# Attention scores and context as 32 by 32 products in runs, in place of block-diagonal 128 by 128 products between projections

## The chip, the core and the metric

The kernel runs on one core of one Trainium2 chip. The metric is the device time of one execution in microseconds; before the change it is 1934.57 (median of three runs, 1934.41 to 1936.26). A core has TensorE (matmuls, and weight loads that the trace keeps apart as PEld), VectorE (DVE), ScalarE (ACT), GpSimd (POOL) and SyncE (SP, which issues DMAs).

## The reference

One layer over 2048 tokens of width 1024, in float32. Attention is inside each token, between its 32 heads of 32 numbers; the feed-forward part has weights that are first rounded to a 16-level code per block of 64.

```
x = hidden                                   # (1, 2048, 1024)
n = layernorm(x)
q, k, v = ((n @ w.T + b).reshape(1, 2048, 32, 32) for w, b in ((wq, bq), (wk, bk), (wv, bv)))
scores  = einsum('bshd,bstd->bsht', q, k) / sqrt(32)
context = einsum('bsht,bstd->bshd', softmax(scores), v)
x = x + context.reshape(x.shape)
h = silu(n2 @ dq(w1).T) * (n2 @ dq(w2).T)    # n2 = layernorm(x), dq: NF4 quantize and dequantize, 2752 rows
x = x + h @ dq(w3).T
```

So each token has two products of 32 by 32 matrices: the scores (32 heads by 32 heads) and the context.

## The kernel before, in words

The 2048 tokens are 16 tiles of 128 (T = 16). After a stage that turns the attention weights (to 65 us), a step per tile runs the attention stage (to about 550 us), and the feed-forward stage follows to the end. Of a step n, TensorE first projects tile n on Q, K and V (`project_one`, m = 0, 1, 2). Each projection is two halves of 512 columns, and each half is 16 float16 matmuls of 128x512 (L1104: 8 parts of the width, times the high and the low part of the normalized x). Between Q and K it turns the next tile's x (`turn`, eight float32 transposes, L281). The same step does the attention of tile n - 1: `score_part` (L1144) and `mix_part` (L1156).

VectorE's 32-by-32 transposes lay a tile out so that each quadrant of 32 partitions holds one token's 32 by 32 matrix, 4 tokens at a time, 32 times (QUAD = 32 slots t, in two halves of 16, HALF). Before the change, ScalarE copies the 4 matrices of a slot from qT, or from the flipped exponentials, to the diagonal blocks of a zeroed 128 by 128 matrix `diag[:, t]` (`place`, L1000, called by `place_q` and `place_probs`: 4 copies per half, one per quadrant). One float32 matmul with that matrix as weights and the slot's kT (or vT) as 32 moving columns then does 4 tokens. GpSimd clears diag once.

The order on each engine is written out by hand. TensorE's small products stand one by one behind the big matmuls: `between` in `project_one` spreads the 32 scores over Q's 32 matmuls, the first 16 mixes over K's second half, and the other 16 over V's first half. Counters (semaphores) carry the waits: q_placed and p_placed from ScalarE, k_ready and v_ready from VectorE, scores_done and context_done back. Scores and contexts use the same two banks of PSUM, so a half's scores also wait until the context before was read (ctx_read).

VectorE evacuates each projection half (L802), subtracts the maxima (L939, L941), flips the exponentials (L956), turns q, k and v (L868, L886, L928), weighs and flips the context (L916, L923), does both layer norms' statistics, and looks for maxima of the feed-forward weights. ScalarE also makes the exponentials (L1048), the high parts of x (L287, L1068) and the first levels of the feed-forward weights' code (L1041, L1043).

The steps are: two written out, a loop of six iterations with two steps each, two more written out (in which the feed-forward stage's first work is fed in, `feed` and `ahead`), and a tail. In the tail the last tile's attention stands among the first feed-forward matmuls (L1907): `attend_last(slot)` is called behind each of 96 of them, and puts the scores at slots 0 to 31 and the mixes at slots 40 to 71 (MIX_FROM = 40). C is 8.

Of the kernel before, what the change touches and what calls it, by code (L numbers as in the profile page):

```python
# [24 lines left out]
P = 128  # L25
QUAD = 32
# [149 lines left out]
def attention(nc, g):  # L176
# [13 lines left out]
    with ExitStack() as mine:  # L190
# [327 lines left out]
        diag = sb("diag", [P, QUAD, P])  # L518
# [7 lines left out]
        diag_zero = sem("diag_zero")  # L526
# [3 lines left out]
        q_placed = sem("q_placed")  # L530
# [6 lines left out]
        p_placed = sem("p_placed")  # L537
# [48 lines left out]
        MIX_FROM = 40  # L586
# [133 lines left out]
        def gpsimd(pool, feed):  # L720
# [69 lines left out]
            pool.memset(diag[:], 0.0).then_inc(diag_zero, 1)  # L790
            straight_steps(step, tail, feed)

        def vector(dve, feed):
# [25 lines left out]
            def step(n, u, it, project=True, normalize=True, attend=True, end=True, feed=None, ahead=None):  # L819
# [44 lines left out]
                if project:  # L864
                    dve.wait_ge(evacuated, 6 * n + 2)
                    if not (it is None and n == 0):
                        dve.wait_ge(q_placed, 2 * n)
                    nc.vector.transpose(qT[:].rearrange("p t h u -> p h t u"),  # L868
                                        qkv[:].rearrange("p (h d) -> p h d", d=HD)).then_inc(q_ready, 1)
# [125 lines left out]
        def scalar(act, feed):  # L995
            def place(half, compact, done):

                part = slice(half * HALF, (half + 1) * HALF)
                for rows in quadrants:
                    last = nc.scalar.activation(diag[rows, part, rows].rearrange("p (t u) h -> p t u h", u=2),  # L1000
                                                compact[rows, half * HALF // 2:(half + 1) * HALF // 2], ACT.Copy)
                last.then_inc(done, 1)

            def step(n, u, it, project=True, normalize=True, attend=True, end=True, feed=None, ahead=None):
                if attend:
                    make_level(n, 0)
                    exponential(n, 0)
                    place_probs(n, 0, end)
# [10 lines left out]
                if attend:  # L1019
                    place_probs(n, 1, end)  # L1020
# [4 lines left out]
                if project:  # L1025
                    place_q(n, 0, attend)
# [4 lines left out]
                if project:  # L1031
                    place_q(n, 1, attend)
# [17 lines left out]
            def place_probs(n, half, end):  # L1050
                act.wait_ge(p_ready, 2 * n + half - 1)
                act.wait_ge(scores_done, 2 * n + half - 1)
                place(half, flipped[:].rearrange("p (t u h) -> p t u h", u=2, h=HEADS), p_placed)

            def place_q(n, half, attend):
                if half == 0:
                    act.wait_ge(q_ready, n + 1)
                if attend:
                    act.wait_ge(context_done, 2 * n + half - 1)
                else:  # L1060
                    act.wait_ge(diag_zero, 1)
                place(half, qT[:].rearrange("p t h u -> p t u h"), q_placed)

# [6 lines left out]
            def tail(feed):  # L1070
                next(feed)
                exponential(T, 0)
                halve2(T - 2)
                place_probs(T, 0, True)
                next(feed)
                exponential(T, 1)
                next(feed)
                place_probs(T, 1, True)
                next(feed)
                halve2(T - 1)  # L1080
                next(feed)
# [3 lines left out]
        def tensor(pe, feed_program):  # L1085
            def project_one(n, u, it, m, with_lo, between=None, share=(0, 2), halfway=None):


                for h in range(2):
                    i = 2 * m + h  # L1090
                    if h == 1 and halfway:
                        next(halfway)
# [10 lines left out]
                    for j, (x, w) in enumerate(passes):  # L1103
# [3 lines left out]
                        slot, slots = h * len(passes) + j, 2 * len(passes)  # L1107
                        if between and share[0] * slots <= 2 * slot < share[1] * slots:
                            between((2 * slot - share[0] * slots) * HALF // slots, (2 * slot + 2 - share[0] * slots) * HALF // slots)

            def step(n, u, it, project=True, normalize=True, attend=True, end=True, feed=None, ahead=None,
                         with_lo=False):
                def score(first, last):
                    score_part(n, end, first, last)

                def mix(first, last):
                    mix_part(n, first, last)

                def mix_second(first, last):
                    mix_part(n, HALF + first, HALF + last)  # L1120
# [13 lines left out]
            def score_part(n, end, first, last):  # L1134

                for t in range(first, last):
# [11 lines left out]
            def mix_part(n, first, last):  # L1148

                for t in range(first, last):  # L1150
# [834 lines left out]
```

## Time and profile before

| | |
|---|---|
| median of three runs | 1934.57 us |
| the profiled execution's own time | 1933.85 us |
| its span in the trace | 1932.1 us |
| TensorE matmuls / weight loads busy | 1883.0 / 1053.0 us |
| VectorE, ScalarE, GpSimd busy | 1730.8, 1542.4, 1256.0 us |
| mean granted TensorE clock | 0.992 |

Matmuls are pipelined: one is recorded from its start to a modelled end, so that neighbours overlap, and the time that one costs the engine is the distance between starts. A timeline row puts neighbouring instructions of one line together (x8) and gives the time from the first one's start to the last one's end. Start times are from the span's start. A loop's or a helper's instructions all have one line.

### The profile page before, as it was taken

What the parts mean: (1) busy time and instruction counts of PE and PEld (TensorE: products, weight loads), DVE (VectorE), ACT (ScalarE), POOL (GpSimd) and SP (SyncE); (2) the same over time, 40 slices, a digit from 0 to 9 for tenths busy, and PEclk for the clock granted to TensorE, in tenths of its full rate; (3) what the DMA queues carried; (4) which work ended last, traced back from release to release, by engine and by line L of the source; (5) the groups of instructions that cost most, each with busy time, mean ns of one, the idle gap of its engine ahead of it and who ended that gap; (6) DMA issues with size and microseconds to landing.
All of it is one profiled execution on the core that took longest, in us unless ns stands there. A gap on an engine that the chain in (4) does not pass through costs nothing.

```text
span 1932.1 us, 30875 instructions
## 1 busy us (share of the span) xinstructions
PE 1883.0 (97%) x10326; PEld 1053.0 (55%) x10326; DVE 1730.8 (90%) x1848; ACT 1542.4 (80%) x1779; POOL 1256.0 (65%) x707
## 2 busy tenths in 40 slices
PE   6899999999989999999999999999999999999998
PEld 5688888888764344444444444444444444444443
DVE  6789888888878999999999999999999999999995
ACT  7366757667568899898898998989989899898881
POOL 0134434343464797887877878778788797786971
PEclk9999999999989999999999999999999999999999
DMA  8435545455286422122122122122122122122114
GB/s 316 142 110 171 166 153 177 137 185 155 79 245 157 143 50 61 44 51 58 43 55 54 43 56 50 46 49 60 43 49 60 43 49 60 43 50 55 39 28 186
DMA packets 252861, 181.69 MB, mean 94 GB/s; under 512 B 177792, under 2 KB 220800, under 8 KB 252800
## 3 DMA queue, kind: packets, MB, share of 16 engines
q1 hardware_dynamic: 221600, 167.28, 30.9%
q10 hardware_dynamic: 31200, 13.64, 2.9%
q8 instruction: 33, 0.54, 0.1%
q14 instruction: 28, 0.23, 0.0%
HBM read 114.29 MB, written 24.12 MB: 72 GB/s over the span
## 4 chain that ended last, share of the span: by engine, by line
PE 64%; DVE 1%; issue 0%; DMA 0%; ACT 0%; SPq 0%; POOL 0%; DVEq 0%
PE bank L1907 42%; PE bank L1935 7%; PE bank L1936 7%; PE bank L1937 7%; PE bank L1933 0%; PE bank L1932 0%; DVE bank L1746 0%; DMA w3T_lo<-half 0%; DVE acc L1811 0%; DVE bank L1744 0%; SPq L1396 0%; DVE w_first L1746 0%; ACT half L1625 0%; ACT signs L1612 0%; DVE hidden L1754 0%
## 5 line engine op out<-in xcount | busy, mean ns | idle before, releaser
L1746 DVE SCALAR_TENSOR_TENSOR bank<-signs,bank 128x1024 f32<-128x1024 int8 (+2 forms) x756 | 920.3, 1217 | 54.6 <-ACT signs L1612 27.9
L1907 PE MATMUL bank<-x2T,w12T 128*128 128x512 f16 x4128 | 906.2, 380 | 11.9 <-DMA x2T<-x_lo_dram 9.0
L1907 PEld LDWEIGHTS bank<-x2T,w12T 128*128 128x128 f16 x4128 | 410.1, 99 | 493.3 <-DMA x2T<-x_lo_dram 9.2
L1612 ACT ACTIVATE signs<-w_first,compare_bias 128x1024 int8<-128x1024 f32 (+1 forms) x588 | 630.6, 1138 | 2.4 <-DVE bank L1746 1.9
L1612 ACT ACTIVATE signs<-w_last,compare_bias 128x1024 int8<-128x1024 f32 (+2 forms) x294 | 314.5, 1119 | 0.8 <-DVE w_first L1746 0.6
L1104 PE MATMUL bank<-wT,xT_hi 128*128 128x512 f16 x768 | 292.2, 381 | 2.4 <-PEq L321 2.4
L1104 PE MATMUL bank<-wT,xT_lo 128*128 128x512 f16 x768 | 292.0, 380 | 0.0
L1935 PE MATMUL bank<-w3T_hi,hT_hi 128*128 128x512 f16 x672 | 255.5, 380 | 7.3 <-DVE acc L1811 4.1
L1936 PE MATMUL bank<-w3T_lo,hT_hi 128*128 128x512 f16 x672 | 255.4, 380 | 0.0
L1937 PE MATMUL bank<-w3T_hi,hT_lo 128*128 128x512 f16 x672 | 255.3, 380 | 0.0
L1526 POOL TENSOR_TENSOR acc<-acc,hidden 128x512 f32<-128x512 f32 x160 | 200.8, 1271 | 28.0 <-ACT hidden L1653 27.2
L1144 PEld LDWEIGHTS bank<-kT,diag 128*128 128x128 f32 x1024 | 173.8, 194 | 15.7
L1653 ACT ACTIVATE hidden<-bank,un_scale 128x512 f32<-128x512 f32 x160 | 109.3, 683 | 87.9 <-PE bank L1937 66.1
L1156 PEld LDWEIGHTS bank<-vT,diag 128*128 128x128 f32 x1024 | 170.3, 190 | 15.0
L1811 DVE SCALAR_TENSOR_TENSOR acc<-bank,un_scale,acc 128x512 f32<-128x512 f32 x192 | 143.4, 747 | 22.6 <-PE bank L1933 11.5
L1520 POOL TENSOR_TENSOR hT_lo<-hidden,hT_hi 128x512 f16<-128x512 f32 (+1 forms) x88 | 101.7, 1157 | 87.7 <-ACT hT_hi L1642 85.1
L1144 PE MATMUL bank<-kT,diag 128*128 128x32 f32 x1024 | 157.8, 236 | 0.0
L1493 POOL TENSOR_SCALAR step_part<-w_first 128x1024 f32<-128x1024 f32 (+1 forms) x42 | 152.4, 3628 | 8.0 <-POOL w_last L1506 2.9
L1156 PE MATMUL bank<-vT,diag 128*128 128x32 f32 x1024 | 155.6, 233 | 0.0
L1502 POOL TENSOR_TENSOR w_first<-w_first,step_part 128x1024 f32<-128x1024 f32 (+1 forms) x42 | 99.0, 2358 | 77.2 <-DVE w_first L1746 77.1
L1104 PEld LDWEIGHTS bank<-wT,xT_hi 128*128 128x128 f16 x768 | 113.0, 147 | 36.2 <-issue 2.5
L1104 PEld LDWEIGHTS bank<-wT,xT_lo 128*128 128x128 f16 x768 | 114.4, 149 | 30.4
(143 smaller groups left out, 2352.2 us busy)
## 6 DMA issues: line engine op xcount, KB each, us to landing
ff_raw<-in_L_ffn_w SPq DMA_DIRECT2D x63, 512.0 KB, 4.5
w_first<-in_L_ffn_w SPq DMA_DIRECT2D x41, 512.0 KB, 3.9
w_last<-in_L_ffn_w SPq DMA_DIRECT2D x19, 512.0 KB, 3.9
x_nat<-in_L_attn_hidden_states SPq DMA_DIRECT2D x16, 512.0 KB, 5.4
x_res<-in_L_attn_hidden_states SPq DMA_DIRECT2D x16, 512.0 KB, 4.6
x<-x_res SPq DMA_DIRECT2D x16, 512.0 KB, 3.0
acc<-x SPq DMA_DIRECT2D x4, 2048.0 KB, 9.1
out<-acc SPq DMA_DIRECT2D x15, 512.0 KB, 2.6
```

The source lines that it names most:

```text
L1104: ins = nc.tensor.matmul(to, x, w, start=j == 0, stop=j == len(passes) - 1)
L1144: ins = nc.tensor.matmul(scores_of(n)[:, t], diag[:, t], kT[:, t // 2, :, t % 2], start=True, stop=True)
L1156: ins = nc.tensor.matmul(context_of(n)[:, t], diag[:, t], vT[:, t // 2, :, t % 2], start=True, stop=True)
L1493: nc.gpsimd.tensor_scalar(step_part[0:rows, 0:cols], w_nat(slot)[0:rows, 0:cols], float(BOUNDS[APART]), 2 * HALF_STEP[APART], ALU.is_gt, A ...
L1526: nc.gpsimd.tensor_tensor(acc[:, st, BANK:], acc[:, st, BANK:], hidden[:, st % 2], ALU.add).then_inc(summed, 1)
L1612: nc.scalar.activation(signs[0:rows, ring(v, k), 0:cols], w_nat(v % SLOTS)[0:rows, 0:cols], ACT.Sign, scale=COMPARE[SUMMED[k]][0], bias=co ...
L1746: V.scalar_tensor_tensor(to, part, HALF_STEP[SUMMED[k]], total, ALU.mult, ALU.add).then_inc(sign_used, 1)
L1811: V.scalar_tensor_tensor(acc[:, st, cols], down_bank(st, h), un_scale[:, 2:3], acc[:, st, cols], ALU.mult, ALU.add).then_inc(down_read[h], 1)
L1907: last = nc.tensor.matmul(dst, w, x[:, toks, c], start=c == 0 and i == 0, stop=c == C - 1 and i == 2)
L1935: nc.tensor.matmul(dst, hT_hi[k, p, toks], w3T_hi[k, p, cols], start=p == 0, stop=False)
L1936: nc.tensor.matmul(dst, hT_hi[k, p, toks], w3T_lo[k, p, cols], start=False, stop=False)
L1937: last = nc.tensor.matmul(dst, hT_lo[k, p, toks], w3T_hi[k, p, cols], start=False, stop=p == GROUP - 1)
```

## The change

Four things change.

1. A slot's product is 4 matmuls, one for each quadrant of 32 partitions, with the quadrant's 32 by 32 matrix of qT (or of the flipped exponentials) as weights, straight from where VectorE left it. `diag`, `place`, `place_q`, `place_probs`, the clearing of diag and the counters q_placed, p_placed and diag_zero go. TensorE waits for q_ready, p_ready and centered in their place.
2. The products are no longer spread between big matmuls. A half's 16 slots are one run of 64 matmuls: the first scores ahead of Q, the second in Q's middle, the first mixes in K's middle, the second behind K.
3. In the tail the scores' halves stand at slots 0 and 8, the mixes' at slots 40 and 56.
4. VectorE's transpose of q waits for no placing.

```diff
-            def place(half, compact, done):
-
-                part = slice(half * HALF, (half + 1) * HALF)
-                for rows in quadrants:
-                    last = nc.scalar.activation(diag[rows, part, rows].rearrange("p (t u) h -> p t u h", u=2),
-                                                compact[rows, half * HALF // 2:(half + 1) * HALF // 2], ACT.Copy)
-                last.then_inc(done, 1)
...
                 if project:
                     pe.wait_ge(x_lo_done, 2 * n + 2)
-                    project_one(n, u, it, 0, with_lo, score if attend else None, (0, 2))
+                    if attend:
+                        score_part(n, end, 0, HALF)
+                    project_one(n, u, it, 0, with_lo, score_second if attend else None)
                 if normalize:
                     pe.wait_ge(normed, n + 2)
                     turn(x_nat[:, 1 - u], x_turned)
                 if project:
-                    project_one(n, u, it, 1, with_lo, mix if attend else None, (1, 2))
-                    project_one(n, u, it, 2, with_lo, mix_second if attend else None, (0, 1), ahead)
+                    project_one(n, u, it, 1, with_lo, mix_first if attend else None)
+                    if attend:
+                        mix_part(n, HALF, QUAD)
+                    project_one(n, u, it, 2, with_lo, ahead_half if ahead else None)
...
-                    if t % HALF == 0:
-                        pe.wait_ge(q_placed, 2 * n + half - 1)
+                    if t == 0:
+                        pe.wait_ge(q_ready, n)
                     if t % HALF == 0 and end and scores_of(n) is scores:
                         pe.wait_ge(ctx_read, 2 * n + half - 3)
-                    ins = nc.tensor.matmul(scores_of(n)[:, t], diag[:, t], kT[:, t // 2, :, t % 2], start=True, stop=True)
+                    if t % HALF == 0:
+                        pe.sem_inc(held, 1)
+                    for rows in quadrants:
+                        ins = nc.tensor.matmul(scores_of(n)[rows, t], qT[rows, t // 2, :, t % 2], kT[rows, t // 2, :, t % 2], start=True, stop=True)
...
                     if t % HALF == 0:
-                        pe.wait_ge(p_placed, 2 * n + half - 1)
-                    ins = nc.tensor.matmul(context_of(n)[:, t], diag[:, t], vT[:, t // 2, :, t % 2], start=True, stop=True)
+                        pe.wait_ge(p_ready, 2 * n + half - 1)
+                        pe.wait_ge(centered, 2 * n + half - 1)
+                    if t % HALF == 0:
+                        pe.sem_inc(held, 1)
+                    for rows in quadrants:
+                        ins = nc.tensor.matmul(context_of(n)[rows, t], flipped[rows, t * HEADS:(t + 1) * HEADS], vT[rows, t // 2, :, t % 2],
+                                               start=True, stop=True)
...
-                    if slot < QUAD:
-                        score_part(T, True, slot, slot + 1)
-                    elif MIX_FROM <= slot < MIX_FROM + QUAD:
-                        mix_part(T, slot - MIX_FROM, slot - MIX_FROM + 1)
+                    if slot in LAST_SCORES:
+                        score_part(T, True, LAST_SCORES.index(slot) * HALF, (LAST_SCORES.index(slot) + 1) * HALF)
+                    elif slot in LAST_MIXES:
+                        mix_part(T, LAST_MIXES.index(slot) * HALF, (LAST_MIXES.index(slot) + 1) * HALF)
```

TensorE at the start of a step inside the loop, before: a weight load goes with each matmul and has no row of its own; L1104 is a projection, L1144 a score.

```order
L1104 MATMUL bank<-wT,xT_hi 128x512 [waits evacuated]
L1141 REGISTER_ALU [waits k_ready]
L1143 REGISTER_ALU [waits q_placed]
L1144 MATMUL bank<-kT,diag 128x32 [waits ctx_read]
L1104 MATMUL bank<-wT,xT_lo 128x512
```

The same place after the change (L1110 is a score, L1066 a projection):

```order
L1106 REGISTER_ALU [waits q_ready,k_ready,x_lo_done]
L1110 MATMUL bank<-kT,qT 32x32 [waits ctx_read]
L1110 MATMUL bank<-kT,qT 32x32 x63
L1058 ISA
L1066 MATMUL bank<-wT,xT_hi 128x512 [waits evacuated]
L1066 MATMUL bank<-wT,xT_lo 128x512
```

Sixteen products that stood between the first half's matmuls of Q are one block of 64 rows ahead of them all.

TensorE in K's middle and behind K, after the change (L1126 is a mix):

```order
L1121 REGISTER_ALU [waits v_ready]
L1126 MATMUL bank<-vT,flipped 32x32 [waits p_ready,centered]
L1126 MATMUL bank<-vT,flipped 32x32 x63
L1066 MATMUL bank<-wT,xT_hi 128x512 [waits evacuated]
...
L1066 MATMUL bank<-wT,xT_lo 128x512
L1126 MATMUL bank<-vT,flipped 32x32 [waits p_ready,centered]
L1126 MATMUL bank<-vT,flipped 32x32 x63
L1058 REGISTER_ALU
```

The second half's mixes stood in V's first half and are now ahead of V.

ScalarE in one step before, from the first exponential to the first level:

```order
L1048 ACTIVATE probs<-probs 128x512 [waits centered]
L1000 ACTIVATE diag<-flipped 32x16x32 [waits scores_done,p_ready]
L1000 ACTIVATE diag<-flipped 32x16x32 x3
L287 ACTIVATE xT_hi<-bank 128x512 [waits x_turned] x2
L1048 ACTIVATE probs<-probs 128x512 [waits centered]
L1068 ACTIVATE x_half<-x_res 128x1024 [waits normed2]
```

And after the change:

```order
L1026 ACTIVATE probs<-probs 128x512 [waits centered]
L287 ACTIVATE xT_hi<-bank 128x512 [waits x_turned] x2
L1026 ACTIVATE probs<-probs 128x512 [waits centered]
L1032 ACTIVATE x_half<-x_res 128x1024 [waits normed2]
```

The copies are gone, and all else keeps its order.

## Rows read from the trace of the kernel before

**Rows 1.** The page: busy us (share) and instructions, and the clock in 40 slices.
```profile
PE 1883.0 (97%) x10326; PEld 1053.0 (55%) x10326; DVE 1730.8 (90%) x1848; ACT 1542.4 (80%) x1779; POOL 1256.0 (65%) x707
...
PEclk9999999999989999999999999999999999999999
```
**Rows 2.** Sums over five steps of 30.67 us, one from 301.44: busy, and means.
```profile
sum 153.35, PE 153.35 PEld 126.19 DVE 135.49 ACT 101.58 POOL 63.83; mean PE 30.67 PEld 25.24 DVE 27.10 ACT 20.32 POOL 12.77
```
**Rows 3.** Groups by line and shape: busy us, mean ns, idle before.
```profile
L1144 PE MATMUL bank<-kT,diag 128*128 128x32 f32 x1024 | 157.8, 236 | 0.0
```
**Rows 4.** Timeline of TensorE inside Q of one step: start us, length us.
```profile
301.80 0.38 PE L1104 MATMUL bank<-wT,xT_lo 128*128 128x512 f16 x1
302.01 0.30 PE L1144 MATMUL bank<-kT,diag 128*128 128x32 f32 x2
302.15 0.38 PE L1104 MATMUL bank<-wT,xT_hi 128*128 128x512 f16 x1
...
302.51 0.38 PE L1104 MATMUL bank<-wT,xT_lo 128*128 128x512 f16 x1
```
**Rows 5.** Timeline of TensorE in streams of one shape.
```profile
72.27 1.04 PE L281 MATMUL bank<-ident,x_nat 128*128 128x128 f32 x8
73.15 0.38 PE L1104 MATMUL bank<-wT,xT_hi 128*128 128x512 f16 x1
60.05 1.06 PE L463 MATMUL bank<-wT 128*128 128x128 f16 x16
62.74 0.16 PE L506 MATMUL bank<-ones,lo_sum 128*1 128x1 f32 x1 [0.70 <-DVE lo_sum L428]
62.74 0.19 PE L506 MATMUL bank<-ones,lo_sum 128*1 128x1 f32 x2 [0.70 <-DVE lo_sum L428]
```
**Rows 6.** Timeline where weights of another height follow, and where not (28.33).
```profile
28.33 0.22 PE L463 MATMUL bank<-wT 128*128 128x128 f16 x1
28.33 0.08 PEld L469 LDWEIGHTS bank<-ident,qkv_top 128*1 128x1 f32 x1
29.76 0.22 PE L463 MATMUL bank<-wT 128*128 128x128 f16 x1
29.91 0.18 PEld L473 LDWEIGHTS bank<-scale_row,ones 1*128 1x128 f32 x1
12.32 0.25 PE L473 MATMUL bank<-scale_row,ones 1*128 1x2 f32 x1
12.49 0.14 PEld L486 LDWEIGHTS bank<-ident,w_raw 128*128 128x128 f32 x1
```
**Rows 7.** Groups by line and shape: ScalarE's copies into diag.
```profile
L1000 ACT ACTIVATE diag<-qT 32x512 f32<-32x512 f32 x128 | 86.1, 673 | 5.5 <-PE bank L1156 2.4 <-DVE qT L868 2.0
L1000 ACT ACTIVATE diag<-flipped 32x512 f32<-32x512 f32 x128 | 80.3, 628 | 56.7 <-DVE flipped L956 36.6 <-issue 18.9
```
**Rows 8.** Timeline of TensorE in the tail.
```profile
551.47 0.38 PE L1907 MATMUL bank<-x2T,w12T 128*128 128x512 f16 x1
569.24 0.61 PE L1907 MATMUL bank<-x2T,w12T 128*128 128x512 f16 x1 [9.04 <-DMA x2T<-x_lo_dram]
588.23 15.70 PE L1907 MATMUL bank<-x2T,w12T 128*128 128x512 f16 x72
```
**Rows 9.** Timeline of VectorE in the step from 301.44.
```profile
312.82 0.70 DVE L956 STREAM_TRANSPOSE flipped<-probs 128x512 f32<-128x512 f32 x1
317.96 0.70 DVE L956 STREAM_TRANSPOSE flipped<-probs 128x512 f32<-128x512 f32 x1
325.45 1.25 DVE L886 STREAM_TRANSPOSE kT<-qkv 128x1024 f32<-128x1024 f32 x1
```
**Rows 10.** Stretch of the lower clock: length, busy of PE, PEld, DVE, ACT, POOL, clock, DMA, GB/s.
```profile
561.80:575.40 13.60, 6.16 (x26) 5.11 (x27) 6.89 (x9) 8.45 (x11) 6.86 (x5) 0.50 1.05 392
```
**Rows 11.** Timeline of TensorE in the last steps.
```profile
513.53 0.27 PE L1953 MATMUL bank<-ident,top 128*4 128x128 f32 x1 [0.90 <-DVE top L1769]
519.91 0.22 PE L1956 MATMUL bank<-ident,ff_raw 4*128 4x4 f32 x1 [2.66 <-DVE ff_raw L1783]
```

More of the change, by code:

```diff
@@ L517, in attention @@
         vT = sb("vT", [P, QUAD // 2, HD, 2])
-        diag = sb("diag", [P, QUAD, P])
         probs = sb("probs", [P, QUAD, HEADS])
@@ L529, in attention @@
         q_ready = sem("q_ready")
-        q_placed = sem("q_placed")
         k_ready = sem("k_ready")
@@ L536, in attention @@
         p_ready = sem("p_ready")
-        p_placed = sem("p_placed")
         context_done = sem("context_done")
@@ L585, in attention @@
         MARKS = 8
-        MIX_FROM = 40
+        LAST_SCORES, LAST_MIXES = (0, C), (5 * C, 7 * C)
         def all_steps(eng, step, tail, feed):
@@ L789, in gpsimd @@
             pool.wait_ge(w_turned, GROUPS * PAIRS)
-            pool.memset(diag[:], 0.0).then_inc(diag_zero, 1)
             straight_steps(step, tail, feed)
@@ L865, in step @@
                     dve.wait_ge(evacuated, 6 * n + 2)
-                    if not (it is None and n == 0):
-                        dve.wait_ge(q_placed, 2 * n)
                     nc.vector.transpose(qT[:].rearrange("p t h u -> p h t u"),
@@ L1007, in step @@
                     exponential(n, 0)
-                    place_probs(n, 0, end)
                 if feed:
@@ L1018, in step @@
                     turn_high2(act, n - 2)
-                if attend:
-                    place_probs(n, 1, end)
                 if end and not feed:
@@ L1024, in step @@
                     make_level(n, 1)
-                if project:
-                    place_q(n, 0, attend)
                 if end and not feed:
@@ L1030, in step @@
                     make_level(n, 2)
-                if project:
-                    place_q(n, 1, attend)
             def make_level(n, i):
@@ L1048, in exponential @@
                 nc.scalar.activation(flat, flat, ACT.Exp, scale=float(1 / np.sqrt(np.float32(HD)))).then_inc(exp_done, 1)
[L1050 to L1062, printed above, removed]
             def halve2(n):
@@ L1073, in tail @@
                 halve2(T - 2)
-                place_probs(T, 0, True)
                 next(feed)
@@ L1077, in tail @@
                 next(feed)
-                place_probs(T, 1, True)
                 next(feed)
@@ L1085, in tensor, with project_one @@
         def tensor(pe, feed_program):
-            def project_one(n, u, it, m, with_lo, between=None, share=(0, 2), halfway=None):
+            def project_one(n, u, it, m, with_lo, halfway=None):
                 for h in range(2):
@@ L1091, in project_one @@
                     if h == 1 and halfway:
-                        next(halfway)
+                        halfway()
                     to = bank[:, (6 * u + i) % PROJ_RING]
@@ L1106, in project_one, with score_second, mix_first, ahead_half @@
                             ins.then_inc(projected, 1)
-                        slot, slots = h * len(passes) + j, 2 * len(passes)
-                        if between and share[0] * slots <= 2 * slot < share[1] * slots:
-                            between((2 * slot - share[0] * slots) * HALF // slots, (2 * slot + 2 - share[0] * slots) * HALF // slots)
             def step(n, u, it, project=True, normalize=True, attend=True, end=True, feed=None, ahead=None,
                          with_lo=False):
[L1113 to L1120, printed above, removed]
+                def score_second():
+                    score_part(n, end, HALF, QUAD)
+                def mix_first():
+                    mix_part(n, 0, HALF)
+                def ahead_half():
+                    next(ahead)
                 if project:
                     pe.wait_ge(x_lo_done, 2 * n + 2)
-                    project_one(n, u, it, 0, with_lo, score if attend else None, (0, 2))
+                    if attend:
+                        score_part(n, end, 0, HALF)
+                    project_one(n, u, it, 0, with_lo, score_second if attend else None)
                 if normalize:
```

1 line of the change is left out of this document (removed).

## The prediction

> **What bounds the kernel now.** I read the page's busy shares and slices first, then the sums over one stretch as long as a step of the attention stage, then TensorE's own timeline inside it, then the tail. TensorE is busy 97% of the span and its granted clock is full nearly throughout [rows 1]. One tile's step takes 30.67 us, and in it TensorE is never idle while VectorE works 27.1 us and ScalarE 20.3 [rows 2]. So 3.6 us is all that TensorE can lose per step before VectorE takes over, and what TensorE gains or loses per step is a change of the span.
>
> What a small product costs TensorE stands in [rows 3, 4]. The trace has 1024 matmuls on L1144 for 512 products (16 tiles of 32 slots), so a float32 product is two passes, each a weight load and a matmul. Projection matmuls with nothing between them start 0.216 us apart (72 in 15.70 us, [rows 8]); with one product between them they start 0.356 apart (301.80, 302.15, 302.51). A product therefore costs 0.140 us. Its parts fit: the first pass's load runs beside the big matmul, the second's does not. A float32 load of 128 columns paces a stream at 0.11 us (eight transposes from 72.27 to the next line's start at 73.15: [rows 5]), so with m for a matmul of 32 moving columns, 0.140 = m + (0.11 − m) + m gives m = 0.030; I take 0.028, a quarter of what a matmul of 128 float32 columns could take at most in the same stream. The step adds up: 96 × 0.216 + 64 × 0.140 + 0.88 for the turn of x_nat = 30.6.
>
> **What the change does, part by part.**
> *Placing.* 256 copies on ScalarE, 166 us in all [rows 7], and POOL's clearing of diag go. ScalarE has 10 us of slack in each step, and TensorE, busy throughout the step, waits for no copy, so I take 0; the cover is TensorE's own work, and were it gone the step would be VectorE's.
>
> *Products.* A slot's product of 128 by 128 weights becomes four of 32 by 32. The order has 64 matmul rows per run; with two passes each that is 128 pairs of load and matmul, and a step has four runs: 512 pairs in place of 128. Within one shape the next load starts when the matmul before it starts (28.33 and 28.33, [rows 6]), and the spacing is the longer of the two: 0.11 for float32 loads of 128 columns, 0.056 for float16 matmuls of 128 columns (16 in 1.06 us, of which the last takes 0.22, [rows 5]). A load of 32 columns should take a quarter of 0.11, 0.027; the matmul stays at 0.028. The nearest row for so small a pair is the sum on L506: two passes of one column, both inside 0.19 where the two passes of 32 columns with 128-column loads need 0.30 [rows 4, 5]; one alone is recorded at 0.16, so they start 0.03 apart. I take 0.028: a run is 128 × 0.028 = 3.58 us. The bounds are 0.007 (the four quadrants wholly side by side) and 0.056 (nothing overlapped, or two instructions never faster than in the float16 stream).
>
> The Trainium skill, "TensorEngine Tiling (Array Packing)", section Instruction Overhead, gives each matmul about 60 cycles however few its columns and warns against splitting a dimension that is already small. An estimate from it at 2.4 GHz is 0.025 us per pair, 3.2 us per run, and the sum below would come out 23 us lower.
>
> *Going in and out of the small shape.* Today all shapes in the attention steps use the whole array. The trace has one change of height, to and from weights of one partition. Into the change it starts 0.15 after the start of a matmul of 0.22, out of it 0.17 after one of 0.25 [rows 6]. So the load waits until some 0.07 us before the matmul's recorded end. Into a run that is 0.38 − 0.07 + 0.03 of load against 0.216, so 0.12 more; out of it 0.19 − 0.07 + 0.03 against 0.03, again 0.12. A run costs 0.24 for both, between 0 (no such stop here) and 0.5. So a run is 3.82 us.
>
> *Per step.* TensorE: 96 × 0.216 + 0.88 + 4 × 3.82 = 36.9; against 30.6 that is 4 × 3.82 − 64 × 0.140 = +6.3 us. Fifteen steps have attention inside: +95 us.
>
> *Waits.* Runs are now queued ahead of whole halves of projections, so a late operand would hold all of TensorE. None is late at this pace. The first half's flipped exponentials end 12.1 us into the step that starts at 301.44, the second's 17.2 [rows 9]; they will be wanted at 18.9 (two runs, Q, the turn, half of K) and 26.1. kT ends 25.3 us into the step, about 2.0 behind K's end, and the next step's scores come 10.7 us after K ends. VectorE's 27.1 us lie inside 36.9. Issue counts on SP and POOL's queues do not change.
>
> *Tail.* The last tile's scores (slots 0 to 31) and mixes (40 to 71) stand in the first feed-forward products. TensorE reaches slot 24 at 560.2, waits 9.04 us for x2T until 569.24, and runs at half clock to 575.4 [rows 8, 10]. With both score runs at slots 0 and 8 it reaches slot 24 after 24 × 0.216 + 7.64 = 12.8 us from 551.47 in place of 8.7, still inside the 17.8 at which x2T lands, so the scores cost nothing and slots 24 to 31 are free of products at half clock. From 569.24 to slot 72 it took 19.0; now 16 slots, mostly at half clock (6.6), then 7.64 + 32 × 0.216 = 14.6: 21.2. The tail adds 2 us.
>
> *Stalls in the last steps.* TensorE waits 0.90 and 2.66 for VectorE's search of the scales [rows 11]. It will come about 3 us later to the first of them, so 1 us goes; the second starts behind the first's answer, so I let it stand. What is late next stays VectorE.
>
> Sum: 95 + 2 − 1 = +96 on the profiled execution's 1933.85 us: **2030 us**. The median of the runs shown is 1934.57, 0.04% above that execution, which is nothing beside the terms.
>
> **The rivals.**
> *A, the forecast:* loads hidden behind matmuls at 0.028 per pair, a stop only at a run's ends. For it: every stream in [rows 5] keeps that law. Against: none there is longer than 24 pairs, while a run is 128. Chance 0.5, with 1990 to 2060 as its own range (no stop and 0.025 per pair; a stop of 0.5).
>
> *B, the supply of instructions or the loads bind:* a pair costs 0.04 to 0.056. No row shows two instructions in less than 0.056 for more than two pairs. At 0.056 a run is 7.4 us, a step +20.7, so 15 × 20.7 + 8 in the tail: 2250. At 0.04, 2125. Chance 0.28.
>
> *C, the other side:* the four quadrants run beside one another, and the change is faster. The runs pay once a pair costs under (64 × 0.140 / 4 − 0.24) / 128 = 0.0156 us. If a slot's four quadrants took the time of one (0.056 for two passes), a run would be 0.9 + 0.24 and TensorE's step 26.2 us; then VectorE's 27.1 binds, a gain of 3.5 × 15 = 52: 1880. If only the second pass of one quadrant lies beside the first of the next, a pair is near 0.016 and the time near 1935. No row shows two matmuls side by side, and no row has a product of that shape. Chance 0.14, of which 0.12 is faster than before.
> The Trainium skill, "TensorE: Matmul & The Clock Gate", section Part 3: Packing small matmuls, has matmuls on different tiles of the array start about 4 ns apart; that rule is this rival, and no run here shows it yet.
>
> *D, a stop between quadrants too:* if each of the 64 quadrant products of a run waits as in [rows 6], it costs 0.12 + 0.03 + 0.03 for its first pass less overlap, about 0.175 with its second: a run 11.2 us, +36 a step, 2475. Chance 0.05. The rest, 0.03, is for small surprises, such as the clock falling in a run. That the edit does not do what it says I leave out: the order shows 64 rows in each of four runs.
>
> **How the numbers follow.** 2030 is A's time. Below 1985 lies C (0.14), above 2200 B's upper end and D (together about 0.08), so 1985 to 2200 holds the time nearly 8 times in 10. Faster by over 0.2% (about what a measurement of this kernel can tell from no change): 0.12, from C. Within it: 0.02. Slower: 0.86, from A, B, D.
>
> **What would show it.** Right: 8192 matmuls of 32 by 32, starting 28 ns apart in a run, each run 3.8 us, a load delayed by 0.1 us at its two ends, a step of 36.9 us with VectorE still at 27, the 9.04 us wait at about 5. B shows as 40 to 56 ns between starts, D as gaps every second pair, C as a step of 27 to 31 us with VectorE waited for. It is wrong if TensorE stands idle at a run's first matmul for p_ready or k_ready, or if the time between starts inside a run is steady and under 20 ns.

## The result, and the profile after

The change makes the kernel 0.56% faster: 1925.05 us median (four executions, 1922.42 to 1925.85) against 1935.41 for the kernel before on the same chip (1934.41 to 1936.59), a ratio of 0.9944 with a 95% interval of 0.9927 to 0.9961. Forecast were 2030 us and a range from 1985, so the prediction is wrong, and on the other side of no change. The profiled execution took 1925.85 us, 8.0 less than the one before.

The page of the kernel after, to be read against [rows 1]: busy us, share and count, the clock in 40 slices, and the queue that brings instructions (packets, MB, share).

```profile
PE 1843.8 (96%) x16470; PEld 889.9 (46%) x16470; DVE 1726.5 (90%) x1848; ACT 1377.9 (72%) x1523; POOL 1252.9 (65%) x706
...
PEclk9999999989989999999999999999999999999999
...
q8 instruction: 106, 1.74, 0.4%
```

The counts are as the order had them: 6144 more matmuls, 256 fewer ScalarE instructions. TensorE is busy 39 us less with them. New are one more slice with a lower clock on the page (slice 8, in the attention stage), and 106 packets of instructions where the profile before had 33 (its row was "33, 0.54, 0.1%").

TensorE's timeline inside one step, in Q's middle (columns as in [rows 4]):

```profile
306.01 0.38 PE L1066 MATMUL bank<-wT,xT_lo 128*128 128x512 f16 x1
306.31 1.29 PE L1110 MATMUL bank<-kT,qT 32*32 32x32 f32 x128
307.53 0.39 PE L1066 MATMUL bank<-wT,xT_hi 128*128 128x512 f16 x1
```

This is the row that decides. 128 matmuls, as counted, take 1.29 us from the first start to the last end. One lasts 0.19 (the source-line view of L1110 has 184/191/258 ns), so they start (1.29 − 0.19) / 127 = 0.0087 us apart, not 0.028. The run costs 307.53 − 306.01 − 0.216 = 1.30 us in place of 3.82. Its ends are about as I sized them: the first small matmul starts 0.30 after the big one (0.38 − 0.07 = 0.31 in my working), and the next big one 0.12 after the last small one (0.19 − 0.07 + 0.03 = 0.15).

With 1.30 in my own sum a step is 96 × 0.216 + 0.88 + 4 × 1.30 = 26.82 us against 30.64, and fifteen steps should gain 57. They gained nothing. The first feed-forward matmul, [rows 8] at 551.47 before, starts at 551.61:

```profile
551.61 0.38 PE L1878 MATMUL bank<-x2T,w12T 128*128 128x512 f16 x1
...
565.73 6.36 PE L1878 MATMUL bank<-x2T,w12T 128*128 128x512 f16 x17 [5.11 <-DMA x2T<-x_lo_dram]
...
579.46 18.95 PE L1878 MATMUL bank<-x2T,w12T 128*128 128x512 f16 x87
```

The 8 us that were gained stand behind that point. Slot 72, 15 matmuls of 0.216 behind the last row's start, comes at 582.7 where [rows 8] have it at 588.23. The other 2.5 us come later, and I didn't follow them up.

Where the 57 went shows in the starts of `turn`. Before, the turns from 98.37 to 466.05 are 30.64 apart. After, they come at 153.55, 187.79, 215.79, 249.36, 277.37, 311.00, 339.01, 372.61, 400.14, 436.58: the steps of the loop are by turns about 28.0 and 33.6 us long (of the long ones, one is 34.2 and one 36.4). Two windows of the kernel after (length, busy and count of PE, PEld, DVE, ACT, POOL, clock, DMA share, GB/s), the first one of the short steps, the second a piece of a long one:

```profile
203.50:231.50 28.00, 27.35 (x618) 14.71 (x617) 27.33 (x37) 9.72 (x11) 12.00 (x7) 1.00 0.59 168
...
297.80:304.60 6.80, 5.71 (x137) 3.25 (x138) 3.41 (x9) 0.17 (x1) 3.67 (x4) 0.50 0.66 236
```

And what lies ahead of that piece, the timeline of TensorE:

```profile
294.55 0.38 PE L1066 MATMUL bank<-wT,xT_lo 128*128 128x512 f16 x1
298.02 1.61 PE L1110 MATMUL bank<-kT,qT 32*32 32x32 f32 x104 [3.09 <-issue]
300.51 0.54 PE L1110 MATMUL bank<-kT,qT 32*32 32x32 f32 x24 [0.88 <-issue]
300.98 0.61 PE L1066 MATMUL bank<-wT,xT_hi 128*128 128x512 f16 x1
```

V's last matmul starts at 294.55. The next step's first product starts 3.5 us later, nothing that the profile shows was awaited ("issue"), and inside that run TensorE stops again, with 24 matmuls to go, where the program has no wait. From the end of the first stop, at 297.8, the granted clock is 0.50 (1.2 of 2.4 GHz) for 6.8 us. The clock is at 0.50 behind the stop of each of the five long steps. The place is the loop's end: the source-line view has the branches of TensorE's sequencer (duration in ns: min/median/max; first and last start). The first row is of the kernel before, the next two of after, of which the last is the feed-forward stage's loop:

```profile
L600 PEldq COMPARE_BRANCH  x6: 76/208/232, 175.4 to 481.8; - x6
```
```profile
L596 PEldq COMPARE_BRANCH  x6: 83/6434/7502, 167.1 to 478.6; - x6
L1293 PEldq COMPARE_BRANCH  x8: 76/208/234, 820.7 to 1691.0; - x8
```

Five of six branches are taken (the sixth leaves the loop, 83 ns). Each taken one lasts 6.3 to 7.5 us where it had lasted 0.21. The one at 291.0 lasts 6.5, to 297.5; TensorE has matmuls queued until 294.55, and only what is longer than that is idle time. The loop's body, two steps, had 2 × (96 + 128 + 8) = 464 matmuls and as many loads, 928 in all (other instructions not counted). Now it has 2 × (96 + 512 + 8) and their loads, 2464, as a window of two steps of the kernel after shows:

```profile
233.34:294.92 61.58, 56.96 (x1233) 30.54 (x1232) 53.27 (x73) 19.82 (x22) 24.85 (x15) 0.94 0.56 166
```

The feed-forward loop, whose body has some 1150, keeps its 0.21. My first theory was therefore **S**: the longer body is no longer at hand when TensorE goes back to its start, so instructions have to be brought again; that costs the idle time, and the idle time costs the clock. The rival, **V**: what is late is data. A step of 28.0 us holds 27.3 us of VectorE's work in the window above, so VectorE would set the time whatever the loop does.

Last the waits of TensorE after (us in total, times, longest):

```profile
PE bank L1110 <- issue: 26.9, 16, 4.1
...
PE bank L1126 <- issue: 8.3, 3, 5.9
...
PE bank L1878 <- DMA x2T<-x_lo_dram: 5.1, 1, 5.1
...
PE bank L281 <- DVE x_nat L275: 2.1, 4, 0.8
PE bank L1924 <- DVE top L1740: 2.1, 1, 2.1
```

35 us of "issue". New among the waits for data in the steps are only x_nat and, once, 0.2 us for the flipped exponentials. A single stop of 5.9 us is in the last steps, in the middle of a run of mixes at 541.83.

### The profile page after: what moved, and what is told of

It reads as the page before. It is cut to its first block and busy times, and to the rows that moved or that the text cites. A ratio compares the mean times of both kernels' runs of the same rounds, so it can differ in the third digit from the quotient of the medians.

```text
span 1924.1 us, 42902 instructions
## 1 busy us (share of the span) xinstructions
PE 1843.8 (96%) x16470; PEld 889.9 (46%) x16470; DVE 1726.5 (90%) x1848; ACT 1377.9 (72%) x1523; POOL 1252.9 (65%) x706
## 5 line engine op out<-in xcount | busy, mean ns | idle before, releaser
L1878 PE MATMUL bank<-x2T,w12T 128*128 128x512 f16 x4128 | 896.5, 380 | 8.1 <-DMA x2T<-x_lo_dram 5.1
L1878 PEld LDWEIGHTS bank<-x2T,w12T 128*128 128x128 f16 x4128 | 404.0, 98 | 497.0 <-DMA x2T<-x_lo_dram 5.6
L1066 PE MATMUL bank<-wT,xT_hi 128*128 128x512 f16 x768 | 301.2, 392 | 2.4 <-PEq L321 2.4
L1066 PE MATMUL bank<-wT,xT_lo 128*128 128x512 f16 x768 | 300.2, 391 | 0.0
L1019 ACT ACTIVATE w12T<-w12T,compare_bias 128x1024 f32<-128x1024 f32 x45 | 51.7, 1148 | 142.1 <-issue 51.5
L1026 ACT ACTIVATE probs<-probs 128x512 f32<-128x512 f32 x32 | 20.1, 629 | 145.8 <-DVE probs L934 145.8
L797 DVE SCALAR_TENSOR_TENSOR qkv<-bank,scales,bias 128x512 f32<-128x512 f32 x96 | 71.4, 743 | 56.6 <-PE bank L1066 55.6
L1066 PEld LDWEIGHTS bank<-wT,xT_hi 128*128 128x128 f16 x768 | 77.0, 100 | 92.7 <-issue 13.2
L1066 PEld LDWEIGHTS bank<-wT,xT_lo 128*128 128x128 f16 x768 | 77.0, 100 | 87.4 <-issue 10.1
L758 POOL TENSOR_TENSOR w12T<-w12T 128x1024 f32<-128x1024 f32 x28 | 66.0, 2359 | 68.7 <-ACT w12T L1021 68.7
```

Source lines behind the costliest of these rows:

```text
L1066: ins = nc.tensor.matmul(to, x, w, start=j == 0, stop=j == len(passes) - 1)
L1878: last = nc.tensor.matmul(dst, w, x[:, toks, c], start=c == 0 and i == 0, stop=c == C - 1 and i == 2)
```

## The experiments

### e1: TensorE's loop written out

```diff
-                middle_steps(pe, step, feed)
+                for n in range(2, T - 2):
+                    step(n, n % 2, None)
+                last_steps(step, feed)
```

> The changed kernel with TensorE's loop of six iterations written out as twelve steps; the other engines and all waits as they are. Theory S (supply of instructions): a run of 128 small matmuls takes 1.3 us, and the gain is given back because the loop's body no longer stays with TensorE's sequencer: its branch takes 6.4 us and TensorE idles 3 us ahead of the first scores, then half clock follows. So without the branch the waits of L1110 on issue fall from 26.9 us to under 10, the stretches at half clock at each second step go, and the time is 1885 to 1900. Rival D (data): the idle is a late kT or a bank that VectorE has not read; then nothing changes, 1920 to 1930.

Measured: 1904.51 us (1903.55 to 1905.96) against 1935.92, ratio 0.9837 (0.9818 to 0.9856). No branch is left on TensorE. Its waits:

```profile
PE bank L1880 <- DMA x2T<-x_lo_dram: 10.1, 1, 10.1
...
PE bank L1110 <- issue: 7.6, 6, 2.2
PE bank L281 <- DVE x_nat L275: 6.7, 11, 1.0
```

Ten steps in one window (182.22 to 464.99, from a turn to a turn) take 28.3 us each with the clock at 1.00:

```profile
182.22:464.99 282.77, 272.15 (x6161) 146.20 (x6161) 268.40 (x366) 99.12 (x110) 125.60 (x70) 1.00 0.61 175
```

So S holds for the long steps, though the time is above the 1885 to 1900 that S had given. It returns 30 us of the attention stage (the first feed-forward matmul comes at 521.4), and the tail takes a part back: x2T comes 24.3 us earlier (541.43 for 565.73), not 30, and is waited for 10.1 us in place of 5.1. The stops inside runs are fewer, not gone; the same 16 KB packets are brought (100 in place of 106), but now in a straight line.

### e8: the same edit in the kernel before (control)

> Control: the kernel before with TensorE's loop written out. Its body was kept whole by the sequencer (branch 0.21 us), so writing it out removes nothing: theory S says 1930 to 1938, with instruction packets up from 33 to about 55. If it falls by 20 us or more, the gain of e1 is not the changed kernel's branch.

Measured: 1935.01 us (1933.32 to 1937.03), ratio 0.9995 (0.9986 to 1.0005). Writing the loop out is worth nothing where the branch costs 0.21 us. The 20 us of e1 are what the change broke, not a gain that had always been there. The packets agree: written out, the kernel before brings 52 in place of 33, so its loop's rounds were not brought anew; the changed kernel brings 106 with the loop and 100 without.

### e2: the kernel before with four steps in the loop's body

```diff
-                middle_steps(pe, step, feed)
+                with pe.Fori(0, LOOP // 2) as it:
+                    for v in range(4):
+                        step(it * 4 + 2 + v, v % 2, it)
+                last_steps(step, feed)
```

> The kernel before, TensorE's loop with four steps per iteration and three iterations in place of two and six: the same instructions executed, none of the change's products, only a body twice as long. Theory S: the body outgrows what is kept, so each of the three branches takes over 1 us in place of 0.21 and instruction packets rise from 33 to 50 or more; TensorE has big matmuls queued that hide most of it, so the time is 1934 to 1945. If such a body is still kept, branches stay at 0.2 us and the limit lies between it and the changed kernel's body. Rival D: branches stay at 0.2 us, time 1935.

Measured: 1941.7 us (1939.17 to 1944.02), ratio 1.0029 (1.0019 to 1.0039), with a body of some 1856 matmuls and loads, two branches taken in place of five, and 55 packets in place of 33. The branches and the wait behind them:

```profile
L1178 PEldq COMPARE_BRANCH  x3: 76/5281/5295, 237.8 to 489.0; - x3
```
```profile
PE bank L1104 <- issue: 3.9, 2, 1.9
```

The old products, untouched, get the new stall from the body's length alone: 5.8 us for two branches, 2.9 each. The branch stays short up to 1150 matmuls and loads and is long at 1856; where in between it changes stays open.

### e3: the slots of one quadrant first, then the next

The same 64 products of a run (128 matmuls), in the other order, so that neighbours are on the same quadrant:

```diff
-                for t in range(first, last):
...
-                    for rows in quadrants:
+                for rows in quadrants:
+                    for t in range(first, last):
```

> The changed kernel with the order inside each run turned over: all 16 slots of one quadrant, then the next quadrant, in place of the four quadrants of each slot. Same matmuls, same counts. Theory P (side by side): the quick spacing of 8.6 ns is four quadrants at once, each of which takes 27 ns per matmul; neighbours in one quadrant then start 27 ns apart, a run takes about 3.6 us in place of 1.3, the step is 36 us and the time 1990 to 2030. Rival Q (a small matmul is short by itself): spacing stays at 8.6 ns, the time at 1925.

Measured, one execution: 2077.86 us, above the 1990 to 2030 expected. A run between two big matmuls is now, in the timeline of TensorE:

```profile
301.69 3.96 PE L1107 MATMUL bank<-kT,qT 32*32 32x32 f32 x128
305.58 0.39 PE L1066 MATMUL bank<-wT,xT_hi 128*128 128x512 f16 x1
```

(3.96 − 0.19) / 127 = 0.0297 us per matmul. That is the law of my forecast and almost its number (0.028): it holds among neighbours on one quadrant. The same 128 matmuls in the order of the change start 0.0087 apart, so the difference is the overlap between quadrants. The four quadrants lie on the array's diagonal, so a neighbour there shares neither rows nor columns; no run has neighbours that share one of the two. e3 also shows what I had not foreseen, a clock that falls with TensorE never idle. Two windows:

```profile
279.90:320.80 40.90, 40.90 (x618) 26.18 (x617) 26.01 (x36) 9.79 (x11) 11.24 (x7) 0.92 0.41 118
306.20:309.60 3.40, 3.40 (x9) 1.21 (x8) 2.12 (x4) 0.00 (x0) 0.00 (x0) 0.50 0.57 154
```

TensorE is busy all of 40.90 us, and two stretches of 3.4 us in it are at half clock. The step is 40.9 where my forecast had 36.9: 4 × (3.98 − 3.82) = 0.6 is the run, and 2 × 1.7 = 3.4 the clock. The loop's body is as long as the change's and brings the same 106 packets, yet a taken branch lasts 3.3 to 3.7 us in place of 6.3 to 7.5, and TensorE's waits on "issue" are 0.3 us in all: here the queued work covers the branch.

### e4: the old block-diagonal products in the new places

Runs of a half tile, with diag, its copies and their counters as before:

```diff
-                        ins = nc.tensor.matmul(scores_of(n)[rows, t], qT[rows, t // 2, :, t % 2], kT[rows, t // 2, :, t % 2], start=True, stop=True)
+                    ins = nc.tensor.matmul(scores_of(n)[:, t], diag[:, t], kT[:, t // 2, :, t % 2], start=True, stop=True)
```

> The kernel before with only the order changed: its 128 by 128 products with diag, placed in the four runs of the changed kernel. Theory: in a run nothing hides the float32 load of 128 columns, so a product costs 2 x 0.109 = 0.22 us in place of 0.140; a step is 64 x 0.08 = 5 us longer, time 2000 to 2020, and no stretch at half clock since the body is as long as before. Rival: the order by itself is what helps (operands ready earlier), time under 1935.

Measured, one execution: 2020.07 us, at the top of the 2000 to 2020 expected. A run in TensorE's timeline (x32 are the two passes of 16 products):

```profile
310.33 3.65 PE L1145 MATMUL bank<-kT,diag 128*128 128x32 f32 x32
313.82 0.38 PE L1104 MATMUL bank<-wT,xT_hi 128*128 128x512 f16 x1
```

From the first product to the next big matmul are 3.49 us, 0.218 per product, where one behind a big matmul costs 0.140 [rows 4]. That is twice the 0.11 at which loads of 128 float32 columns pace a stream [rows 5], as if no load lay beside a big matmul any more. So gathering them was not what made the change good; with the old products it costs 84 us. This body has no more instructions than before's (33 packets), and no stop at the loop's end appears. Against the expectation, the clock is at 0.50 here too, for 3.4 us at a time, every 37 to 54 us, with TensorE busy:

```profile
295.30:298.70 3.40, 3.40 (x10) 1.24 (x9) 0.95 (x2) 3.33 (x6) 2.08 (x1) 0.50 0.56 163
```

### e5: the new products in the old places

The quadrant products of a slot (8 matmuls) behind each big matmul, where the old ones stood; the loop and its length are the change's.

```diff
-                        halfway()
+                        next(halfway)
...
+                        slot, slots = h * len(passes) + j, 2 * len(passes)
+                        if between and share[0] * slots <= 2 * slot < share[1] * slots:
+                            between((2 * slot - share[0] * slots) * HALF // slots, (2 * slot + 2 - share[0] * slots) * HALF // slots)
```

> The changed kernel's 32 by 32 products in the places of the kernel before: one slot (8 matmuls) behind each big matmul. The first profile shows a load into a run held until 0.31 us after the big matmul's start (0.22 without a run) and 0.12 out of it. Theory W (a stop at every change of shape): a slot costs 0.09 + 2 x 0.03 + 0.12 = 0.27 us in place of 0.140, a step is 64 x 0.13 = 8.5 us longer than before, time 2050 to 2090, and the waits on issue are gone because instructions are wanted more evenly. Rival: the stop is paid once per projection half or not at all, time 1880 to 1935.

Measured, one execution: 2078.56 us. TensorE's timeline in Q:

```profile
299.68 0.39 PE L1066 MATMUL bank<-wT,xT_hi 128*128 128x512 f16 x1
300.00 0.26 PE L1109 MATMUL bank<-kT,qT 32*32 32x32 f32 x8
300.20 0.39 PE L1066 MATMUL bank<-wT,xT_lo 128*128 128x512 f16 x1
```

From one big matmul to the next 0.52 us, less 0.216: a slot costs 0.30, of which 8 × 0.0087 = 0.07 are the products and 0.23 the two changes of shape. That is the 0.24 of my working, confirmed on 64 places per step. This loop has the change's long body as well, and what it adds is hidden again: the branch, and all of L1066's waits on "issue" (total, times, longest):

```profile
L596 PEldq COMPARE_BRANCH  x6: 79/3290/3572, 206.6 to 616.8; - x6
```
```profile
PE bank L1066 <- issue: 0.5, 2, 0.3
```

So in these runs the long body costs time only where TensorE gets through its queued work before the branch is done. Why the branch itself is shorter here stays open.

The 0.23 is also why the change needs both of its halves: small products without runs lose 142 us, runs without small products lose 84, the two together gain 10.

### e6: e1 without the row maxima, and e7: the kernel before without them

To test V, e6 is e1 without VectorE's two passes per half that find and subtract the row maxima (the exponentials are taken of the scores themselves). That part of the softmax is left out in e7 and e10 too. In all three ScalarE's exponentials then wait for scores_done and ctx_ready; in e6 and e10, not in e7, its first levels also wait for level_ready. No run has these waits by themselves.

```diff
-                if attend:
-                    center(n, 0)
...
-                if attend:
-                    center(n, 1)
```

> e1_unrolled without the subtraction of each row's largest score ahead of the exponential (softmax is the same without it while scores are small): ScalarE's exponential reads the scores' bank, and VectorE loses four instructions of 0.69 us per step, 2.8 us. Theory V: with the loop written out, a step is bound by VectorE (27.1 us of work against TensorE's 26.8; TensorE waits for x_nat in 11 steps, 6.7 us); without it the step falls from 27.7 to 26.9 us and the waits of L281 on VectorE vanish: 15 to 25 us less in all against 1904.5, with the tail's chain shorter too, 1880 to 1895. Rival: the remaining time is the supply of instructions, then 1900 to 1905.

> Control: the same omission in the kernel before, where TensorE is never idle in a step. Theory V: nothing in the steps, 1925 to 1936 (only waits in the last steps and the tail can shrink). If it gains as much as e6 against e1, VectorE was not what bound e1.

Measured: e6 1898.1 us (1894.48 to 1898.97), ratio 0.98 (0.9783 to 0.9816). e7 1933.42 (1931.8 to 1935.34), ratio 0.9987 (0.9977 to 0.9996). So in the kernel before the omission is worth 2.7 us. e6 lies between the ranges of both theories (1880 to 1895 and 1900 to 1905). Its steps stayed near 28.0 although VectorE had four operations less in each, 2.7 us. By itself this was inconclusive, because another VectorE operation grew. The source-line view of L275, the normalization of the next tile's x that `turn` waits for, of e1 and of e6:

```profile
L275 DVE TENSOR_SCALAR x_nat<-x_nat,mean_var,rstd x16: 792/1450/1592, 56.0 to 463.3; 128x1024 f32<-128x1024 f32 x16
```
```profile
L275 DVE TENSOR_SCALAR x_nat<-x_nat,mean_var,rstd x16: 794/2879/2891, 55.9 to 459.8; 128x1024 f32<-128x1024 f32 x16
```

The minimum, 0.79, is what it takes alone. In most steps of e6 it starts together with a GpSimd product and ends after it (the timeline):

```profile
431.88 2.34 POOL L758 TENSOR_TENSOR codes<-codes,w12T 128x1024 f32<-128x1024 f32 x1
431.90 2.88 DVE L275 TENSOR_SCALAR x_nat<-x_nat,mean_var,rstd 128x1024 f32<-128x1024 f32 x1
```

This gave a third theory: not VectorE's total, but the place of L275 in its order. It stands behind Q's first evacuation and the first maxima, and in steps of 28 us the turn comes for it too early.

### e9: e1 with the normalization moved ahead

```diff
+                if normalize and attend:
+                    norm_apply(dve, n + 1, 1 - u)
                 if project:
                     evacuate(n, u, it, 0, 0)
...
-                if normalize and attend:
-                    norm_apply(dve, n + 1, 1 - u)
```

> e1_unrolled with one VectorE instruction moved: the scaling of the next tile's x (L275) ahead of the evacuation of Q's first half and of the scores' maxima, in place of behind them. In e1 TensorE waits for it ahead of the eight transposes in 11 steps, 6.7 us. Theory C (the chain from x_nat binds the step, not VectorE's total): these waits go to under 1 us and the time falls by 5 to 12 us, to 1893 to 1900. Theory V (VectorE's total work of 27.1 us binds): the wait turns up at another operand and the time stays within 3 us of 1904.5.

> e6_no_max with the same move. In e6 the omission freed 2.8 us of VectorE per step, but L275 grew from 1.45 to 2.88 us: it now starts together with GpSimd's addition L758 and ends with it. Moved ahead it should take 0.8 us again, TensorE's waits for it (5.3 us) vanish, and a step come to 27.0 to 27.3 us in place of 28.0: 1884 to 1892 against 1898. If the steps stay at 28.0, instructions are what is late.

Measured: e9 1895.71 us (1893.0 to 1898.07), ratio 0.9792 (0.9775 to 0.9808). It computes all of the reference and is the fastest such kernel here, 39 us ahead of the kernel before. L275 takes 0.8, and TensorE waits for it no more:

```profile
L275 DVE TENSOR_SCALAR x_nat<-x_nat,mean_var,rstd x16: 792/814/815, 56.4 to 459.6; 128x1024 f32<-128x1024 f32 x16
```

e10, the same move in e6: 1887.54 us (1885.07 to 1891.18), ratio 0.9758 (0.9742 to 0.9775). Ten steps of each, e9 and then e10:

```profile
182.76:463.78 281.02, 272.45 (x6161) 148.21 (x6160) 263.93 (x368) 98.73 (x111) 129.91 (x71) 0.99 0.61 176
```
```profile
179.76:451.68 271.92, 269.63 (x6161) 146.98 (x6160) 237.94 (x326) 96.51 (x110) 131.39 (x71) 1.00 0.63 182
```

e10's steps are 27.2 on average and mostly 26.89, beside the 26.82 of the sum. Four of e9's ten are 26.9 to 27.04 too, with the maxima done. The others have stops, none of them put down to data. e9's waits of TensorE from 130 to 480 us:

```profile
PE bank L1110 <- issue: 6.8, 5, 1.9
PE bank L1066 <- issue: 2.2, 3, 0.9
PE bank L1126 <- issue: 1.4, 1, 1.4
```

So V falls: in these four steps VectorE's total costs at most the 0.15 us between 26.89 and 27.04. Most of the gap between e9 and e10 is stops for "issue": 10.4 us here, 5.0 in e10 over the same stretch, and one step of e9 at a lower clock after its longest. Why e10 has fewer stays open. They sit in the middle of runs and of projections, where the program waits for nothing, as a late instruction would. That they are the supply of instructions is argued from that place and not shown; no run removed them.

## Why the prediction was wrong

**What bounds the kernel** was right: TensorE, with VectorE 3.6 us behind per step. It is TensorE's idle time, not its work, that the kernel after adds.

**Products: the step that failed.** The prediction had "the spacing is the longer of the two" and so 0.028 us per pair. Every stream in [rows 5, 6] has neighbours that share rows and columns of the array, and I carried their law over to neighbours that share none. e3 measures the law where it holds, 0.0297, and the timeline after measures it across quadrants, 0.0087. The term 4 × 3.58 us should have been 4 × 1.1. That is 15 × 4 × 2.5 = 150 us of the forecast. My nearest row was near in size (one column, two passes) and not in kind, and I said of rival C that "no row shows two matmuls side by side". That made the row's absence into evidence; it was only absence. The 8.7 ns are far under the 15.6 ns at which I had the runs begin to pay, and under the steady 20 ns that I had named as a sign of being wrong.

The Trainium skill, "TensorE: Matmul & The Clock Gate", Part 3: Packing small matmuls, has matmuls on different tiles start about 4 ns apart. This case's 8.7 ns, sustained over 128 of them, each with its load, is twice that. The Trainium skill, "TensorEngine Tiling (Array Packing)", Instruction Overhead, has about 60 cycles per matmul; an estimate from it at 2.4 GHz is 25 ns. As a distance between starts it does not hold across tiles here (8.7 ns); within one the 29.7 ns do not contradict it.

**In and out of the small shape** was right: 0.24 forecast, about 0.2 by the run's own sum and 0.23 in e5.

**Placing** was put at 0. No run takes the copies away by themselves, so that term is not tested.

**Per step.** +6.3 us forecast. The sum with the measured run is −3.8, which e10 reaches. What the kernel after shows is −2.6 in a short step, and +3.0 in a long one.

**Waits.** "None is late" was wrong in the small: once the step is 28 us, x_nat is late by up to 0.8 us, and 1.0 in e1. "None" was worked out for a step of 36.9 alone, though a rival had one of 27. A reading was off as well: kT ends 3.8 us behind K's last matmul before (it ends at 326.70, and V begins at 322.92), not about 2.0; the 10.7 us of room cover that too. VectorE as the bound, which I gave to rival C, did not come: C's 1880 us assumed a step of 27.1 without a stop.

**Supply of instructions.** Rival B named it, as a price per pair. It came at the loop's branch instead, which had no place in my sum. The accounts of the attention stage close with it: of 57 us expected, five taken branches take back 31 (the long steps less 28.0: 6.2, 5.6, 5.6, 5.6, 8.4), fifteen steps at 28.0 in place of 26.82 take 18, and the stop of 5.9 us in the last steps most of the rest. Of the 1.2 us in each step, e9 and e10 show two parts: x_nat's place in VectorE's order, and stops on "issue". I had counted the added matmuls as time on TensorE only. Their instructions also have to be brought, and the page has a row for that queue. The branch's cost depends on the pace too, and not on the body's length alone: in e3 and e5 the same body costs next to nothing.

**Tail.** x2T's wait was forecast at about 5 and measured 5.1, and that is luck: TensorE came to slot 24 after 9.0 us in place of 12.8, since the score runs are short, and x2T landed after 14.1 us in place of 17.8 (565.73 − 551.61). The two errors cancel. From slot 24 to slot 72 it took 17.0 us (565.73 to 582.7), not 21.2: both mix runs cost about 1.3 us in place of 3.82, and 1.24 us of a stop come back. They ran at full clock, which had returned at 570.8. At half clock small matmuls start about 13 ns apart, by the 104 in 1.61 us above. The 17.0 are 2.0 us less than before, and x2T landing 3.5 us earlier (565.73, not 569.24, [rows 8]) makes up the 5.5 found above.

**Stalls in the last steps.** 0.90 and 2.66 before [rows 11] are 2.06 and 0.98 now, for top and ff_raw: 0.5 us less in sum, not the 1 forecast, and spread otherwise.

## What to carry to other kernels

Price a small matmul by where its neighbour sits: on another quadrant it is nearly free (8.7 ns here), on the same one it costs the whole spacing (29.7), and each change between small and full weights costs some 0.1 us, so small products pay in runs whose neighbours alternate quadrants. Count instructions as well as microseconds: when an edit multiplies the instructions of a loop's body, compare the branch's duration and the packets of the instruction queue before and after, and write the loop out if the branch has grown and idle time on "issue" stands behind it. When the bound gets 10% faster, read again every wait that used to have some slack, since orders on other engines were tuned to the old step.

## Unexpected behaviour of the hardware

- A loop's taken branch on TensorE lasts 0.21 us with bodies of 928 and 1150 matmuls and loads, 5.3 us with 1856 and 6.3 to 7.5 with the change's 2464. Behind the latter TensorE is idle for 3.8 to 6.1 us, with 6.8 us or more at half clock. With the same 2464 in e3 and e5, where a step takes 41 us, it lasts 3.3 to 3.7 us and TensorE is idle for 0.3 and 0.5 us in all.
- TensorE's clock fell to 0.50 with no idle time before it: in e3 twice in a step of 40.9 us, in e4 every 37 to 54 us, mostly for 3.4 us. In e5, with the same small products as the change but spread among big ones, it stays at 1.00:

```profile
270.00:310.00 40.00, 39.93 (x613) 19.34 (x611) 24.80 (x36) 8.67 (x10) 12.17 (x7) 1.00 0.40 120
```

  Both kernels where it falls have long runs of narrow matmuls, 3.6 to 4 us each. What in them does it was not tried.
- VectorE's normalization of x (L275, 128x1024 float32) takes 0.79 us alone, 1.56 in most steps of the kernel before (at 310.21 it runs beside the last 1.0 us of a GpSimd product), and 2.88 when a GpSimd product of 2.34 us starts with it.
